# Layer 0's FFN in a four-layer gated cross-attention kernel: LayerNorm statistics by ScalarE's accumulator, the offset step in two parts, the value folding in other steps

## The reference, cut to what matters

```python
def fp4_quant_dequant(x):
    xb = x.reshape(shape[:-1] + (shape[-1] // 16, 16))
    scale = jnp.max(jnp.abs(xb), axis=-1, keepdims=True) / 6.0
    scale = jnp.maximum(scale, jnp.float32(1e-12))
    xn = xb / scale
    idx = jnp.searchsorted(_MID, jnp.abs(xn))
    q = _GRID[idx] * jnp.sign(xn) * scale
    return q.reshape(shape)

def fp4_linear(x, w):
    return jnp.einsum('bsk,nk->bsn', fp4_quant_dequant(x), fp4_quant_dequant(w))

gate = fp4_linear(x, w_gate)          # 256 -> 704
y = fp4_linear(x, w_up)               # 256 -> 704
return fp4_linear(silu(gate) * y, w_down)

x = x + tanh(g_ffn[0]) * _L0_ffn_ref(_layernorm(x), w_gate, w_up, w_down)
```

## Time and profile before

| | us |
|---|---|
| median of 3 runs | 1131.84 (1128.95 to 1134.78) |
| the profiled execution | 1129.75 |
| its span, first to last instruction | 1128.0 |
| stage of layer 0's FFN | 95.3 to 267.8 |
| busy in the whole span: PE, PEld, DVE, ACT, POOL | 1058.1, 903.9, 787.9, 518.8, 163.9 |

### The profile page before, as it was taken

How to read it: one execution, slowest core, us unless ns; L and a number is a source line. 1 busy time by engine, 2 the same in 40 slices (tenths; PEclk the granted TensorE clock), 3 DMA queues, 4 the chain that set the end, 5 groups by cost and what they waited for, 6 DMA issues and landing times.

```text
span 1128.0 us, 18809 instructions
## 1 busy us (share of the span) xinstructions
PE 1058.1 (94%) x6238; PEld 903.9 (80%) x6238; DVE 787.9 (70%) x1809; ACT 518.8 (46%) x1196; POOL 163.9 (15%) x227
## 2 busy tenths in 40 slices
PE   4877899998999989998999997999989999999998
PEld 4755567776999968887888886999868888888887
DVE  5787879997788655547888875887656574565544
ACT  3666544333555455554455452566542333333322
POOL 2241000001121052221111001133321010010000
PEclk9898999999999989999999999999989999999999
DMA  9401010002000000000000005000021222121220
GB/s 284 101 1 41 1 12 1 1 1 75 1 0 1 1 12 1 0 1 1 2 0 0 1 1 238 1 0 1 1 62 62 62 70 57 58 84 43 71 84 29
DMA packets 30374, 41.19 MB, mean 37 GB/s; under 512 B 13615, under 2 KB 19577, under 8 KB 29414
## 3 DMA queue, kind: packets, MB, share of 16 engines
q1 hardware_dynamic: 29437, 39.63, 11.4%
q10 hardware_dynamic: 873, 0.72, 0.3%
HBM read 37.80 MB, written 2.54 MB: 36 GB/s over the span
## 4 chain that ended last, share of the span: by engine, by line
PE 51%; DVE 2%; ACT 1%; DMA 0%; issue 0%; POOL 0%; POOLq 0%; DVEq 0%; SPq 0%; ACTq 0%
PE psum L2011 16%; PE psum L2022 8%; PE psum L1398 6%; PE psum L1376 5%; PE psum L1213 3%; PE psum L1171 2%; PE psum L349 2%; PE psum L1386 2%; PE psum L1195 1%; PE psum L1184 1%; PE psum L1415 1%; PE psum L1983 1%; PE psum L861 0%; PE psum L1973 0%; PE psum L1436 0%
## 5 line engine op out<-in xcount | busy, mean ns | idle before, releaser
L298 POOL TENSOR_TENSOR rstd<-ve,mhalf 128x1 f32<-128x1 f32 x128 | 83.5, 654 | 705.5 <-DVE ve L293 705.5
L360 ACT COPY work<-psum 128x256 f32<-128x256 f32 (+2 forms) x241 | 99.4, 438 | 138.6 <-PE psum L349 133.5
L349 PE MATMUL psum<-ident,work 128*128 128x128 f32 (+2 forms) x596 | 95.4, 281 | 16.1 <-DVE xT_lo L1300 4.3
L2096 ACT CAST h_hi<-work 128x512 fp32r<-128x512 f32 x68 | 42.2, 621 | 124.7 <-DVE work L2166 88.6
L2156 DVE TENSOR_TENSOR work<-psum,work 128x512 f32<-128x512 f32 x68 | 46.9, 689 | 72.4 <-ACT work L2088 72.2
L349 PEld LDWEIGHTS psum<-ident,work 128*128 128x128 f32 (+2 forms) x596 | 72.7, 146 | 30.1 <-DVE xT_lo L1300 6.2
L2011 PE MATMUL psum<-x_hi,ew_hi 128*128 128x512 f32 (+1 forms) x272 | 87.1, 402 | 0.2 <-ACT work L2088 0.2
L1597 PE MATMUL psum<-early,work 128*128 128x352 f32 x256 | 82.0, 475 | 3.3 <-ACT zone L572 2.8
L2011 PE MATMUL psum<-x_hi,ew_lo 128*128 128x512 f32 (+1 forms) x272 | 84.8, 393 | 0.0
L2011 PE MATMUL psum<-x_lo,ew_hi 128*128 128x512 f32 (+1 forms) x272 | 84.8, 393 | 0.0
L2022 PE MATMUL psum<-ew_hi,h_hi 128*128 128x256 f32 x272 | 76.3, 281 | 2.5 <-DVE h_lo L2173 2.4
(11 more groups left out here) (269 smaller groups left out, 2559.8 us busy)
## 6 DMA issues: line engine op xcount, KB each, us to landing
work<-expert_shares SPq DMA_DIRECT2D x64, 256.0 KB, 3.2
early<-in_experts_in SPq DMA_DIRECT2D x1, 6528.0 KB, 19.0
x<-in_x_in SPq DMA_DIRECT2D x4, 512.0 KB, 7.3
early<-in_W_in SPq DMA_DIRECT2D x2, 1024.0 KB, 5.9
out_x<-x SPq DMA_DIRECT2D x3, 512.0 KB, 4.5
early<-in_Wk SPq DMA_DIRECT2D x1, 1024.0 KB, 6.7
early<-in_Wq SPq DMA_DIRECT2D x1, 1024.0 KB, 9.2
zone<-in_Wv SPq DMA_DIRECT2D x1, 1024.0 KB, 13.6
```

What stands on the lines that cost most here:

```text
L298: pool.tensor_tensor(rstd[:, slot:slot + 1], ve[:, slot:slot + 1], mhalf[:, 0:1], ALU.pow).then_inc(s["rstd_ready"], 1)
L349: last = pe.transpose(dst[0:rows, at:at + n], src, ident[0:n, 0:n])
L360: act.copy(dst, src).then_inc(s["tr_copied"], 1)
```

## The change

Three things are changed in this stage, for tiles 2 to 15 (the first two tiles' statistics still come from the stage before).

1. The statistics move from DVE to ACT: a copy whose accumulator sums the row, a 128x1 instruction for minus the mean, and a Square with that as bias whose accumulator gives the squared spread. POOL makes variance + eps, the root and `nmr` from them, three small instructions for one. DVE's `ln_stats` and `nmr` product go.
2. Where a step has both x and h columns, the offset is done in two parts, 256 columns and 704: two instructions for one on ACT (L1646) and on DVE (L1717, L1718).
3. Steps 0 to 3 fold two value units each instead of one, and the last unit is folded in step 9, not in step 13.

```diff
-        VO_RAMP = {-2: 4, -1: 2}
-        VO_LAST = B * KT - sum(VO_RAMP.values())
+        VO_RAMP = {-2: 4, -1: 2, 0: 2, 1: 2, 2: 2, 3: 2}
+        VO_LAST = 4 + B * KT - sum(VO_RAMP.values())
...
+        def offset_parts(t):
+
+            return ([(0, D)] if has(t + 3) else []) + ([(D, QW)] if has(t) else [])
+
         def ffn0_scalar(act):
-            s, tr = f_s[0], Count()
+            s, tr, own = f_s[0], Count(), Count(set_s["scalar_chain"])
+
+            def statistics(t):
+                slot = t % 2
+                total, negmean, spread = (small[:, 8 + 2 * n + slot:9 + 2 * n + slot] for n in range(3))
+                act.activation(xn[1], xt(t), ACT.Identity, accum_out=total).then_inc(set_s["scalar_chain"], 1)
+                act.wait_ge(set_s["scalar_chain"], own.up())
+                act.activation(negmean, total, ACT.Identity, scale=-1.0 / D).then_inc(set_s["scalar_chain"], 1)
+                act.wait_ge(set_s["scalar_chain"], own.up())
+                act.activation(xn[1], xt(t), ACT.Square, bias=negmean, accum_out=spread).then_inc(s["stat_ready"], 1)
...
                 if has(t) or has(t + 3):
-                    a, z = 0 if has(t + 3) else D, QW if has(t) else D
                     act.wait_ge(s["m_ready"], t + 4)
-                    act.activation(mq[:, a:z], mq[:, a:z], ACT.Relu, bias=minus_magic[:],
-                                   scale=MAGIC_E2M1).then_inc(s["r_ready"], 1)
+                    for a, z in offset_parts(t):
+                        act.activation(mq[:, a:z], mq[:, a:z], ACT.Relu, bias=minus_magic[:],
+                                       scale=MAGIC_E2M1).then_inc(s["r_ready"], 1)
...
+                if has(t + 5) and not led(t + 5):
+                    statistics(t + 5)
                 if t in (-4, -3):
                     take_fold(-2, (2 * t + 8, 2 * t + 9))
...
-                if has(t + 5) and not led(t + 5):
-                    ln_stats(dve, t + 5, 1 - p, s)
...
-                    dve.wait_ge(s["r_ready"], t + 4)
-                    link(dve, dve.scalar_tensor_tensor(y, m, MAGIC_E2M1, y, ALU.add, ALU.add))
-                    link(dve, dve.scalar_tensor_tensor(y, y, MAGIC_E2M1, m, ALU.subtract, ALU.subtract))
+                    for b, e in offset_parts(t):
+                        yb, mb = yq[p][:, b:e], mq[:, b:e]
+                        dve.wait_ge(s["r_ready"], offsets.up())
+                        link(dve, dve.scalar_tensor_tensor(yb, mb, MAGIC_E2M1, yb, ALU.add, ALU.add))
+                        link(dve, dve.scalar_tensor_tensor(yb, yb, MAGIC_E2M1, mb, ALU.subtract, ALU.subtract))
...
-                if has(t + 5):
+                if has(t + 5) and led(t + 5):
                     slot = 1 - p
                     dve.wait_ge(s["rstd_ready"], t + 6)
...
                 if has(t + 5) and not led(t + 5):
-                    ln_root(pool, t + 5, 1 - p, s)
+                    slot = 1 - p
+                    negmean, spread = (small[:, 8 + 2 * n + slot:9 + 2 * n + slot] for n in (1, 2))
+                    wait(pool, s["stat_ready"], t + 6)
+                    settle(pool, pool_waits_taken)
+                    pool_link(pool, pool.tensor_scalar(ve[:, slot:slot + 1], spread, 1.0 / D, EPS, ALU.mult, ALU.add))
+                    pool_link(pool, pool.tensor_tensor(rstd[:, slot:slot + 1], ve[:, slot:slot + 1], mhalf[:, 0:1],
+                                                       ALU.pow))
+                    pool.tensor_tensor(nmr[:, slot:slot + 1], negmean, rstd[:, slot:slot + 1],
+                                       ALU.mult).then_inc(s["nmr_ready"], 1)
```

More of the change, by code:

```diff
@@ L255, in link, with pool_link @@
             dve.wait_ge(chain, chain_n.up())
+        pool_chain_n = Count(pool_chain)
+        pool_chain_n.base = 4
+        def pool_link(pool, instruction):
+            instruction.then_inc(pool_chain, 1)
+            pool.wait_ge(pool_chain, pool_chain_n.up())
         def settle(eng, taken=vector_waits_taken):
@@ L265, in flamingo @@
         FRONT = ("stat_ready", "rstd_ready", "xn_ready", "tr_filled", "tr_copied")
-        set_s = stage_sems("setup", "filled", "read", "prep", "wq_scaled", "kb_hi_done", "kb_lo_done", "vp_zero",
+        set_s = stage_sems("setup", "filled", "read", "prep", "wq_scaled", "kb_hi_done", "scalar_chain", "vp_zero",
                            "vb_ready")
@@ L558, in vo_units @@
         def vo_units(t):
-            return VO_RAMP.get(t, 0) if isinstance(t, int) and t < 0 else int(not isinstance(t, int) or t < VO_LAST)
+            return VO_RAMP.get(t, 0) if isinstance(t, int) and t < 4 else int(not isinstance(t, int) or t < VO_LAST)
         def fold_values(pe, dst, bb, k):
@@ L623, in key_split_vector @@
             dve.tensor_tensor(kb_lo[l][:, cols], kb_raw[l][:, cols], kb_hi[l][:, cols].bitcast(F32),
-                              ALU.subtract).then_inc(set_s["kb_lo_done"], 1)
+                              ALU.subtract)
         def key_split_pool(pool, l, n):
@@ L1679, in ffn0_vector @@
         def ffn0_vector(dve):
-            s, tr = f_s[0], Count()
+            s, tr, offsets = f_s[0], Count(), Count()
             def step(t, p):
@@ L1732, in step @@
                                              ALU.mult, ALU.mult).then_inc(s["nmr_ready"], 1)
-            pipeline(dve, -5, step, [(tr, 6 + 2), (chain_n, 2 * (4 + 2 + 2))], T + 2, 5)
+            pipeline(dve, -5, step, [(tr, 6 + 2), (chain_n, 2 * (4 + 2 + 2)), (offsets, 4)], T + 2, 5)
             end_stage(dve, "dve")
@@ L1744, in step @@
                 if has(t + 5) and not led(t + 5):
-                    ln_root(pool, t + 5, 1 - p, s)
-            pipeline(pool, -3, step, [(Count(), 0)], T + 1, 5)
+                    slot = 1 - p
[7 more added lines that the diff above has]
+                                       ALU.mult).then_inc(s["nmr_ready"], 1)
+            pipeline(pool, -3, step, [(pool_chain_n, 4)], T + 1, 5)
             lead_pool(pool, a_s[1])
```

2 lines of the change are left out of this document (1 added, 1 removed).

## The result

| us | before | changed |
|---|---|---|
| median (lowest to highest), 14 runs of each | 1131.05 (1127.09 to 1136.38) | 1126.61 (1123.15 to 1129.72) |
| ratio, 95% interval | | 0.9957 (0.9937 to 0.9977) |
| profiled execution, its span | 1129.75, 1128.0 | 1123.15, 1121.3 |
| stage of layer 0's FFN | 95.3 to 268.9 | 95.4 to 268.4 |

The changed kernel is faster by 0.43%: less than the 0.5% that I called a difference, but the interval leaves no change out, and the median lies 0.4 us under the low end of the forecast range, 5.2 us under the forecast. In this table and from here on the stage is counted to TensorE's first score product of the attention behind it (L1184 of the kernel before), 268.9 us before; that is 1 us after the first instruction of that attention, in either kernel.

The account below looks back on a forecast made before the run. VectorE was taken to bound steps 5 to 12, TensorE next, and a ScalarE-TensorE copy chain steps -1 to 4. Terms +3.4 - 2.1 - 0.7 - 0.6 = 0.0 gave no change, 1131.8 us, range 1127.0 to 1136.0.

Parts of the forecast that it names:

- Steps 5 to 9: Steady steps of layer 0's FFN: from 9.74 us a step to TensorE's 9.32, together -2.1 us.
- The new wait: In each of steps 5 to 9, VectorE waits 0.27 us for ScalarE's offset part of 256 columns.
- Steps 10 to 12: Later FFN steps: -0.3 us in step 10 and -0.19 each in 11 and 12, together -0.7 us.
- The stage's end: End of layer 0's FFN: VectorE's 0.63 us wait for its last-but-one product goes, -0.6 us.
- The price of a fold: TensorE in steps 10 to 13: 0.43 us a pair of matmul records, seven pairs, 3.0 us leaving.
- Statistics on ScalarE: ScalarE's three statistics instructions per tile take 1.7 us, hidden in steady steps; VectorE loses 1.02 us a step.
- The upper bound: ScalarE's three statistics instructions: at most 2.5 us, with each sum read back by a small instruction of 0.38.
- Steps -1 to 4: Early FFN steps, a chain of ScalarE copies and TensorE: +3.9 us at the same clock, +3.4 taken.
- A: Steps -1 to 4: folds hide in TensorE's idle time, early part no longer than now; 1127.4 us, chance 0.18.
- B: Steps 5 to 9 don't shrink, as VectorE and TensorE push each other; 1133.9 us, chance 0.12.
- C: ScalarE's statistics are dear, at 3.5 us for the three paid in steps -1 to 3; 1138.3 us, chance 0.10.
- D: Second offset part not covered by the first if ScalarE starts it 0.3 later; 0.1 us a step, 1132.8, chance 0.05.

Follow-up runs that it names:

- no_fold: The changed kernel with the value folds placed as in the kernel before; median 1129.67 us, ratio 0.9984 to the kernel before.
- ctl_before: The kernel before, unchanged, run against itself; median 1129.42 us, ratio 0.9981.
- late_folds: Changed kernel with step -1's statistics behind the awaited copy, 1, 1, 0, 2 folds in steps 0 to 3, last in step 13; 1125.93 us, ratio 0.9971.

## Why the prediction was wrong, point by point

**The step that failed** is the last one of the sum: 0.0 in one stage was taken for 0.0 in the kernel, with all later stages fixed. The stage gave 0.6 us in the first pair of traces and nothing in the mean of all; the later stages gave 6.2 and 4.6, with their granted clock. A smaller part is the base: of the 5.2 us between forecast and median 0.8 come from taking 1131.84, the median of three runs, for the kernel before, which has 1131.05 over fourteen. "It is wrong ... if another stage moves at all": all five differ, by 0.7 to 3.4 us. The rows for a better bound were there: the two stretches at 0.51 were treated as part of the stage's chain and priced, but the clock row of the profile's page has two slices below nine tenths behind the stage as well, at about 395 and 818 us, and the three runs shown lay 5.8 us apart. The low end, 1127.0, had room for the stage alone.

**Steps 5 to 9**, -2.1 forecast: -1.44 measured, 47.21 for 48.65. VectorE in step 9 of the changed kernel, from its product to the next:

```profile
191.71 0.88 DVE L1712 TENSOR_TENSOR work<-psum,work 128x704 f32<-128x704 f32 x1
...
195.89 0.66 DVE L1726 TENSOR_SCALAR work<-work 128x960 int32<-128x960 int32 x1
196.46 0.48 DVE L1730 SCALAR_TENSOR_TENSOR x<-psum,tg,x 128x256 f32 x1
197.12 0.43 DVE L1739 SCALAR_TENSOR_TENSOR work<-work 128x256 f32<-128x256 f32 x1 [0.18 <-ACT work L1666]
197.58 0.42 DVE L1740 SCALAR_TENSOR_TENSOR work<-work 128x256 f32<-128x256 f32 x1
198.13 0.89 DVE L1739 SCALAR_TENSOR_TENSOR work<-work 128x704 f32<-128x704 f32 x1
199.06 0.89 DVE L1740 SCALAR_TENSOR_TENSOR work<-work 128x704 f32<-128x704 f32 x1
...
201.16 0.88 DVE L1712 TENSOR_TENSOR work<-psum,work 128x704 f32<-128x704 f32 x1
```

The step is 9.45 us, not 9.30. The statistics and the `nmr` product are gone, as predicted. The new wait is there and has its size: from L1730's start to L1739's it is 0.66 us, 0.26 more than the 0.40 without one. What I had not counted is 0.1 at the second part's wait: 197.58 to 198.13 is 0.55, while outside the loop, where the count waited for is a constant, the same pair takes 226.02 - 225.56 = 0.46:

```profile
225.10 0.42 DVE L1739 SCALAR_TENSOR_TENSOR work<-work 128x256 f32<-128x256 f32 x1 [0.18 <-ACT work L1666]
225.56 0.43 DVE L1740 SCALAR_TENSOR_TENSOR work<-work 128x256 f32<-128x256 f32 x1
226.02 0.89 DVE L1739 SCALAR_TENSOR_TENSOR work<-work 128x704 f32<-128x704 f32 x1
```

In the loop the count comes from a register: at 198.05 the trace has a register instruction of VectorE's sequencer (0.04 us) at this wait, and no such one before 226.02. The pair takes 0.55 in all six steps of the loop and 0.46 in all others that have it. The rest, some 0.05 a step, I can't place.

**Steps 10 to 12**, -0.7 forecast: -0.66. **The stage's end**, -0.6: 30.86 to 30.26, and the wait of the earlier trace rows is gone. That term was right for the kernel as a whole; for what the fold move does in it, it was too small. Without the move it is +2.2 (33.10 in `no_fold`), since steps 5 to 12 got faster while TensorE did not. The price of a fold was 0.43 us a pair there; the earlier trace rows show 0.60 for the two records, and only the step from two records (0.70) to four (1.13) below gives 0.43.

**Statistics on ScalarE**, 1.7 us forecast for the three. Step -1 of the changed kernel:

```profile
107.61 0.59 ACT L1676 ACTIVATE work<-x,small,rstd 128x256 f32<-128x256 f32 x1
108.11 0.40 ACT L1645 ACTIVATE work<-x 128x256 f32<-128x256 f32 x1
108.41 0.19 ACT L1645 ACTIVATION_READ_ACCUMULATOR work<-x 128x1 f32 x1
108.63 0.20 ACT L1647 ACTIVATE small<-small 128x1 f32<-128x1 f32 x1
108.87 0.51 ACT L1649 ACTIVATE work<-x,small 128x256 f32<-128x256 f32 x1
109.28 0.19 ACT L1649 ACTIVATION_READ_ACCUMULATOR work<-x,small 128x1 f32 x1
109.37 0.35 ACT L367 COPY work<-psum 128x256 f32<-128x256 f32 x1
```

From 108.11 to 109.47 it is 1.36 us, and the copy behind starts 1.26 after the first. The upper bound had the right shape (each sum is read back by an instruction of its own) and the wrong size: a read-back is 0.19 us, not 0.38. The Trainium skill (ScalarE: Activation LUTs, "What ACT_TABLE_LOAD costs") gives by its formula 0.40, 0.19 and 0.49 us for the three ACTIVATEs; the trace agrees with 0.40, 0.20 and 0.51, and adds the two read-backs. By the rule of the Trainium skill (ScalarE: Activation LUTs, "Rules for kernel authors") to do additions and products on VectorE, the change goes the wrong way. The traces don't bear that out for the steady steps: 1.1 us less on VectorE, which sets the pace, against 1.36 on an engine that then has 26.56 busy us of 47.20; with the statistics alone steps 5 to 9 take 47.76 us for 48.65 to 48.69.

**Steps -1 to 4**, +3.4 forecast. The first trace gives +2.1 (67.96 for 65.83), with one stretch at the low clock against two. The second stretch cost the kernel before 1.6 us (64.19 in `ctl_before`, without it in that place), where the prediction put about 1. Taken off, the early part grew by 3.8 us; the sum "if the clock is as before" had 3.9. The mean over five and six traces, 69.4 for 65.5, gives +3.9 too, with 10.2 us of low clock in three of the changed kernel's five traces. TensorE in the changed kernel:

```profile
109.78 0.70 PE L575 MATMUL psum<-zone,early 128*128 128x256 f32 x2 [2.10 <-ACT work L367]
...
118.16 1.13 PE L575 MATMUL psum<-zone,early 128*128 128x256 f32 x4
121.39 1.13 PE L575 MATMUL psum<-zone,early 128*128 128x256 f32 x4 [2.10 <-ACT zone L502]
122.98 1.45 PE L1604 MATMUL psum<-early,work 128*128 128x352 f32 x4 [0.46 <-ACT zone L579]
```

The chain is the one described: the second fold of step 0 waits for its bank behind the key copies, runs 1.13 us (0.87 was counted), its copy follows, and gate and up begin at 122.98 for 120.88, 2.0 later when the stage's starts are laid together; 2.4 was forecast to that point. `late_folds` shows the price of the place: 61.4 us for 67.8 with one or two units fewer in each of steps 0 to 2.

**The rivals.** A (the early chain absorbs the work) is excluded: the early part grew in all five traces. Its number, 1127.4, is near the measured median, but by another mechanism: that would be luck. B (the steady steps don't shrink) is excluded by 47.21 for 48.65. C (statistics dear) is excluded by 1.36 us. D (the second part not covered) has its 0.1 us a step, but not its cause: the trace puts no wait on ScalarE there, and outside the loop the 0.1 is gone.

## What to carry to other kernels

Before a change of a few us is called neutral or good, ask how long each *unchanged* stage is in several traces of the same kernel: here the spread of the untouched five stages, 857.6 to 863.3 us, was larger than every term of the sum. Look at the granted clock of every execution, not only at the two traces: it told more than eleven traces did. Price a stage from its own rows, but take the range from the spread of the whole. And when one engine of a balanced pair is relieved, the other's loose work shows at the end: the moved folds were worth 0.9 us there before the relief and 2.8 after it. Where they are put decides the rest: among the copies of steps 0 to 4 they cost 3.3 us in the kernel before, and with the placing of `late_folds` the way to step 5 is the shortest of all kernels here, 61.4 us.

## What the runs showed of the hardware

- An accumulating ACTIVATE is followed by an ACTIVATION_READ_ACCUMULATOR of 0.19 us on a 128x1 result (185 to 193 ns in all 28 of the first trace of the changed kernel).
- Two executions of one kernel differ in where TensorE's clock is at its lower level: 3.4 or 10.2 us of it in the early part of the same stage, 130.5 or 133.0 us for the same unchanged third stage, and 129.6 or 134.1 for the sixth.
- On VectorE a wait for a count held in a register, in a loop, left 0.55 us from start to start (547 to 549 ns, six steps in each of three traces) where the same pair with a constant left 0.46 (458 to 461 ns).
- Whether an execution has much or little of the lower clock can differ between two kernels whose stages behind the change are the same: 42 of 113 executions at a mean granted clock of 0.972 or lower, and 0 of 39.
